# Activations kept in PSUM, and three weight remainders moved from VectorE to GpSimd

## What is computed

```python
# block 1 of the reference: 4 experts, the token id picks one
g = silu(h @ Wg[e].T); u = h @ Wu[e].T
y = (g * u) @ Wd[e].T            # kept where expert_ids == e
# block 2: 8 experts of 176, a router picks two
topk_s, topk_i = top_k(h @ Wg.T, 2); probs = softmax(topk_s)
y += w[..., e] * ((silu(h @ W1[e].T) * (h @ W2[e].T)) @ W3[e].T)
```

## Time and profile before

| | before |
|---|---|
| median of 3 runs | 164.85 us |
| the profiled execution's own time | 164.04 us |
| its span | 162.2 us |
| TensorE busy | 154.5 us (95%) |
| VectorE busy | 111.7 us (69%) |
| ScalarE busy | 67.8 us (42%) |
| GpSimd busy | 57.2 us (35%) |

### The profile page before, as it was taken

How to read it: one execution, slowest core, us unless ns; L and a number is a source line. 1 busy time by engine, 2 the same in 40 slices (tenths; PEclk the granted TensorE clock), 3 DMA queues, 4 the chain that set the end, 5 groups by cost and what they waited for, 6 DMA issues and landing times.

```text
span 162.2 us, 2463 instructions
## 1 busy us (share of the span) xinstructions
PE 154.5 (95%) x904; PEld 131.0 (81%) x904; DVE 111.7 (69%) x224; ACT 67.8 (42%) x121; POOL 57.2 (35%) x50
## 2 busy tenths in 40 slices
PE   7999899899999999999999799999999999999991
PEld 2477698789897788888889488888888888888890
DVE  0878999785986756799999947917444744444453
ACT  3385775754618622474335812324222222222210
POOL 0679956469767480555467310000000000000000
PEclk9999999999999999999999999999999999999999
DMA  3976353032030003033000000000000300000003
GB/s 107 349 246 191 82 203 107 0 97 76 29 97 0 2 0 101 0 97 97 0 4 0 0 0 2 4 0 0 0 0 4 129 0 0 0 2 4 0 0 129
DMA packets 4620, 8.76 MB, mean 54 GB/s; under 512 B 768, under 2 KB 1408, under 8 KB 4608
## 3 DMA queue, kind: packets, MB, share of 16 engines
q1 hardware_dynamic: 4176, 8.34, 16.3%
q10 hardware_dynamic: 432, 0.27, 0.5%
HBM read 7.55 MB, written 1.05 MB: 53 GB/s over the span
## 4 chain that ended last, share of the span: by engine, by line
PE 65%; DVE 21%; issue 4%; ACT 4%; POOL 3%; DVEq 0%; ACTq 0%; POOLq 0%
PE z L685 36%; PE y L710 22%; DVE act L587 5%; PE z L720 4%; DVE act_lo L552 4%; DVE norm L485 2%; DVE w_lo L558 2%; POOL gated L337 2%; DVE stats L468 2%; DVE hT_lo L492 1%; ACT act_hi L388 1%; ACT silu L416 1%; POOL rstd L299 1%; PE y L627 1%; DVE x_sb L498 1%
## 5 line engine op out<-in xcount | busy, mean ns | idle before, releaser
L685 PE MATMUL z<-hT_hi,w_hi 128*128 128x512 f32 x120 | 47.4, 395 | 1.1 <-ACT hT_hi L362 0.9
L685 PE MATMUL z<-hT_hi,w_lo 128*128 128x512 f32 x120 | 47.1, 393 | 0.0
L710 PE MATMUL y<-w_hi,act_lo 128*128 128x256 f32 x152 | 43.5, 286 | 1.0 <-DVE act_lo L552 0.9
L552 DVE TENSOR_TENSOR act_lo<-act,act_hi 128x512 fp32r<-128x512 f32 x38 | 33.6, 884 | 14.8 <-ACT act_hi L388 14.5
L710 PE MATMUL y<-w_hi,act_hi 128*128 128x256 f32 x152 | 43.0, 283 | 0.0
L710 PE MATMUL y<-w_lo,act_hi 128*128 128x256 f32 x152 | 42.9, 283 | 0.0
L416 ACT ACTIVATE silu<-z 128x512 f32<-128x512 f32 x38 | 22.6, 595 | 41.1 <-PE z L685 41.1
L685 PE MATMUL z<-hT_lo,w_hi 128*128 128x512 f32 x120 | 37.3, 392 | 0.0
L289 POOL TENSOR_TENSOR w_lo<-raw,w_hi 128x768 fp32r<-128x768 f32 (+1 forms) x15 | 27.5, 1845 | 20.3 <-ACT w_hi L353 18.9
L388 ACT CAST act_hi<-act 128x512 fp32r<-128x512 f32 x38 | 23.4, 617 | 19.7 <-DVE act L587 19.4
L710 PEld LDWEIGHTS y<-w_hi,act_lo 128*128 128x128 f32 x152 | 29.0, 191 | 3.2 <-DVE act_lo L552 1.5
(11 more groups left out here) (52 smaller groups left out, 80.8 us busy)
## 6 DMA issues: line engine op xcount, KB each, us to landing
raw<-weights_dram SPq DMA_DIRECT2D x11, 384.0 KB, 3.1
raw<-weights_dram SPq DMA_DIRECT2D x8, 256.0 KB, 4.5
x_sb<-x_dram SPq DMA_DIRECT2D x4, 256.0 KB, 4.4
out_dram<-x_sb SPq DMA_DIRECT2D x2, 256.0 KB, 2.5
out_dram<-x_sb SPq DMA_DIRECT2D x2, 128.0 KB, 2.0
out_dram<-x_sb ACTq DMA_DIRECT2D x2, 128.0 KB, 2.1
consts_sb<-consts_dram SPq DMA_DIRECT2D x1, 68.0 KB, 3.7
ids_sb<-token_ids_dram ACTq DMA_DIRECT2D x1, 4.0 KB, 3.9
```

The costliest lines, as they stand in the source:

```text
L552: nc.vector.tensor_tensor(act_lo[:, i, :], act[:, i, :], act_hi[:, i, :].bitcast(F32), ALU.subtract)\
L685: return nc.tensor.matmul(bank[:], w[b][:, c, cols], tokens[:, h, k, :], **flags)
L710: last = nc.tensor.matmul(o, a[:, q % BUFFERS, rows], w[b][:, c, wd], start=(first and j == 0), stop=(c == CHUNKS[b] - 1 and j == 2), skip ...
```

## The change

- Block b = 0: act(q) is written over its z bank in PSUM, and act_hi and act_lo read it from there.
- Block b = 1: gated(q) is written over the second z bank, and act(q) reads it there; act(q) itself stays in SBUF.
- The waits of up(q) follow: in b = 0 and for q = 16 and 17 it waits for act_lo in place of act (up(16) for act_lo(13), up(17) for act_lo(15)), and from q = 18 on for act(q-2) in place of silu and gated.
- On VectorE act_lo(15) moves ahead of gated(16).
- The remainders of w (0,5), (0,6) and (0,7) are taken by GpSimd and no longer by VectorE.
- rstd for the second half of b = 0 is computed by GpSimd in step 2, not 1.
- The router product for the second half of b = 1 stands behind down(20), not ahead of it.

```diff
-    "inverse_deviation": (1, 3, 4),
+    "inverse_deviation": (2, 3, 4),
-    "scores": (None, (7, 0), (7, 0)),
+    "scores": (None, (7, 0), (7, 1)),
-VECTOR_LO = ((0, 0), (0, 5), (0, 6), (0, 7))
+VECTOR_LO = ((0, 0),)
+        def act_place(q):
+            return z_banks(q)[0][:] if STEPS[q][0] == 0 else act[:, q % BUFFERS, :]
-                nc.scalar.copy(act_hi[:, q % BUFFERS, :], act[:, q % BUFFERS, :]).then_inc(act_hi_done, 1)
+                nc.scalar.copy(act_hi[:, q % BUFFERS, :], act_place(q)).then_inc(act_hi_done, 1)
-                nc.vector.tensor_tensor(act_lo[:, i, :], act[:, i, :], act_hi[:, i, :].bitcast(F32), ALU.subtract)\
+                nc.vector.tensor_tensor(act_lo[:, i, :], act_place(q), act_hi[:, i, :].bitcast(F32), ALU.subtract)\
+                if q == FIRST[1, 0]:
+                    act_low(q - 1)
                 if b == 1:
...
-                    nc.vector.tensor_tensor(gated[:, i, :], gate[:, h, :], z_banks(q)[1][:], ALU.mult)\
+                    nc.vector.tensor_tensor(z_banks(q)[1][:], gate[:, h, :], z_banks(q)[1][:], ALU.mult)\
                         .then_inc(gated_done, 1)
-                if q >= 1:
+                if q >= 1 and q != FIRST[1, 0]:
                     act_low(q - 1)
...
-                factor = z_banks(q)[0][:] if b == 0 else silu[:, i, :]
-                nc.vector.tensor_tensor(act[:, i, :], gated[:, i, :], factor, ALU.mult).then_inc(act_done, 1)
+                factors = (gated[:, i, :], z_banks(q)[0][:]) if b == 0 else (z_banks(q)[1][:], silu[:, i, :])
+                nc.vector.tensor_tensor(act_place(q), *factors, ALU.mult).then_inc(act_done, 1)
...
                 if q >= len(z) and b == 0:
-                    pe.wait_ge(act_done, q - len(z) + 1)
+                    pe.wait_ge(act_lo_done, q - len(z) + 1)
                 elif b == 1 and q < FIRST[1, 0] + 2:
-                    pe.wait_ge(act_done, 2 * q - FIRST[1, 0] - 2)
+                    pe.wait_ge(act_lo_done, 2 * q - FIRST[1, 0] - 2)
                 elif b == 1:
-                    pe.wait_ge(silu_done, q - 1)
-                    pe.wait_ge(gated_done, q - 1)
+                    pe.wait_ge(act_done, q - 1)
```

## The result

The changed kernel takes 167.49 us (median of 4 runs, 166.56 to 168.08), the kernel before 164.75: a ratio of 1.0167, 95% interval 1.011 to 1.0224. It is slower, and 167.49 lies 0.2 us from the predicted 167.7. The sum behind that number holds errors of opposite sign, and that the two numbers lie so close is partly luck, as the rows show.

A forecast was written before the change was run, and what follows sets the result against it. TensorE was taken to bound the kernel, so only its idle time could change. Terms -0.2, +0.8, +2.75, +0.7 and -1.15 summed to +2.9 us on 164.04, or 166.9; with 0.8 for the median 167.7, range 165.9 to 169.2.

The forecast's parts named there:

- R2: Rival: TensorE's clock falls after the pauses before up(17) and up(18), half speed losing 1.9 us: 169.6; chance 0.08.
- (c): Before up(17): it waits for act_lo(15), which stands behind the router's work on VectorE: +2.75 us, 2.6 to 2.95.
- (d): Before up(18): it waits for act(16) in place of gated(16): +0.7 us, bounds 0.6 to 0.8.
- (e): Later up-projections of block 1 wait for act(q-2), with time to spare: cost 0, at most 0.3 us.
- (f): Second router product: its move behind down(20), or an earlier hT_lo, removes the pause there: -1.15 us with the restart.
- (b): Block 0: added pieces make GpSimd set the pace, new pauses before down(3) and the token transposes: +0.8 us at up(8).
- (a): Block 0's activation in PSUM: act_lo never blocked, 0.69 us; -0.8 us before down(1), -0.2 before down(11).
- R1: Rival: GpSimd is not the pace in block 0, both new pauses vanish: sum +1.2 us, 166.1; chance 0.13.
- R3: Rival: VectorE's freed port pays for everything, early pauses vanish and router work shrinks: down to 163.8 us; chance 0.03.
- R4: Rival: the wait before up(17) isn't real, act_lo(15) being done before the router: +0.15 us, 165.0; chance 0.04.

The follow-up runs named there:

- e4: Changed kernel, but VectorE takes the remainders of w (0,5), (0,6), (0,7) again and GpSimd's rstd stands in step 1: 165.85 us, ratio 1.007.
- e8: Kernel before, nothing in PSUM; only act_lo(15) ahead of gated(16), and up(16) and up(17) waiting for act_lo: 168.82 us, ratio 1.0272.
- e6: e5 with gated of block b = 1 in SBUF again, up(q) waiting for silu and gated: 160.94 us, ratio 0.9812.
- e7: e5 with the second router product ahead of down(20) again: 161.47 us, ratio 0.984.
- e10: The changed kernel unaltered, measured a second time: 168.02 us, ratio 1.0227.
- e3: Changed kernel with 12 discarded warm-up matmuls on TensorE in the pause ahead of up(17): 166.21 us, ratio 1.0093.
- e11: e8 with 12 discarded warm-up matmuls in the pause ahead of up(17): 166.76 us, ratio 1.0141.
- e1: Changed kernel, but act(15) stays in its SBUF tile, so up(17) waits for act(15) again: 163.37 us, ratio 0.9922.
- e2: Changed kernel, but act_hi(15) ahead of tanh on ScalarE and act_lo(15) ahead of best_two on VectorE: 163.23 us, ratio 0.9915.
- e5: Changed kernel with the edits of e2 and e4 together: 161.87 us, ratio 0.9859.
- e9: Kernel before, with only the three remainders of w moved to GpSimd and rstd in step 2: 165.34 us, ratio 1.0053.

## Why the prediction was right

The number was right, and so were the largest term and the direction. One of its own signs of being wrong came true all the same: matmuls after the long pause stand 0.43 us apart (R2 below). By its own steps:

- **(c), the wait before up(17): right.** Predicted +2.75 us; the start moved by 2.84 in the profile, the idle time is 2.67 or 2.68 in the four profiles that have it (changed kernel twice, e4, e8), and e8 shows it with nothing else changed. What carried it was reading two orders against each other: up(17) waits for act_lo(15), which stands behind work that itself waits for transposes behind up(16).
- **(d), up(18): right.** Predicted +0.7; 0.56 in the profile, and e6 takes 0.73 back by the chain (0.93 by the medians).
- **(e) right at 0**: no pause after up(18). **(f) right**: -1.15 predicted, -1.17 measured from up(18) to the end, and either edit alone does it (e6, e7).
- **(b), GpSimd's load: the mechanism was right, half of its effect was not there.** Walked: gated(3) to 23.6, act(3) at 23.6, a pause of 0.9 before down(3). Measured: gated(3) ends at 24.1, or at 23.8 in e10, whose up(0) starts at 9.94; the idle time is 1.07 on the weight loads, and from up(6) to up(7) it is 3.72 us against 2.82, 0.90 more. But the second pause, at the token transposes, did not come. I had norm and GpSimd's gated(6) meet with gated(6) first; norm was first (VectorE's timeline, then GpSimd's):

```profile
27.21 1.54 DVE L489 TENSOR_SCALAR norm<-x_sb,mv,rstd 128x256 f32<-128x256 f32 x2
```

```profile
26.99 1.29 POOL L341 TENSOR_TENSOR gated<-silu,gate 128x512 f32<-128x512 f32 x1 [0.42 <-ACT silu L420]
28.50 1.40 POOL L341 TENSOR_TENSOR gated<-silu,gate 128x512 f32<-128x512 f32 x1 [0.22 <-ACT silu L420]
```

 The two norm operations end at 28.75, ahead of the transposes' turn. The text named this as open by 0.1 us and took half of it. From up(7) to up(8) it put some +0.7 us, and it is +0.23 (4.68 against 4.45, in e10 too).
- **(a), PSUM in block 0: under-sized.** I gave it -0.8 and -0.2. The -0.2 for the pause before down(11) counted its idle time alone; from up(8) to up(16) the changed kernel takes 24.54 us against 25.07, in both profiles, so -0.53. With the pieces left on VectorE (e4) up(16) starts at 55.48 where it was 56.92, although that execution's up(0) came 1.0 later: at least -1.4, since the pause before up(8) goes too. That pause stays, as forecast, with the pieces on GpSimd (0.83 us). Taken together, (a) and (b) were put at +0.6 up to up(16) and came to +0.05, and in e10's profile to -0.26. The mis-sized terms are the half of the second pause and the down(11) term.
- **R2, the falling clock: given 8 in 100, and it is what happens most of the time.** It was priced at 1.9 us, half speed over the 3.8 us of two pauses; the clock took 1.57 in the profile, and nothing at up(18). The sum left this term out. The argument against it, that the clock stayed full over pauses of 0.6 to 1.1 us, says nothing of a pause of 2.7. Over the kernels with the unfilled pause (changed kernel twice, e4, e8) 17 of 23 executions show a clock of 0.99 or less; with the pause filled (e3, e11) none of 12, without it (e1, e2, e5, e6, e7) none of 25. Why it falls in most executions and not in the others stays open.

In the profiled execution the errors add up as follows: +2.9 forecast, block 0 -0.55, (c) +0.09, (d) -0.14, the restart and the clock behind the long pause +1.82, (f) -0.02, in all +4.1. They do not cancel there. Against the kernels before beside them the medians are +2.74 (167.49) and, with the same code, +3.77 (e10). That the first lies so near +2.9 is partly luck: two of its four executions kept the full clock, and block 0 was put too high. The executions with a full clock, 166.56, 167.27 and 167.17, are what the sum of +2.9 was about; they lie 1.8 to 2.9 us over the kernel before beside them. Of R1 half is true: one of the two new pauses is absent, the other is there, and e4 and e9 show what GpSimd's load costs. R3 did not hold (the router's work is as long as before, 60.27 to 63.77), nor did R4.

An operation of VectorE with two SBUF inputs is held up beside GpSimd again, 1.83 us in e4 and 2.37 in e6 against 0.69. The Trainium skill, "GPSIMD Engine Reference", section 1 (Specifications), names contention with such instructions, and these rows agree. Taking them off the port is worth over a microsecond in block 0 (e4); in b = 1 it is worth the router product's pause (e7), and nothing once that product has moved (e6). The small variance operation, with one SBUF input, is held up too (1.33 against 0.16, e8). VectorE writing PSUM takes 0.69 to 0.70, as assumed.

## What to carry to other kernels

Where a result is written over its input in a PSUM bank, the bank is free one reader later. Find who reads last, and what stands ahead of that reader in its engine's order: a wait that costs nothing in the steady loop cost 2.8 us at the one step where other work stands in between, and moving the reader and the rounding ahead of it (e2) turned a loss of 1.7% into a gain of 0.85%. Take the parts of such a change apart: here block 0 in PSUM gains, the router product's move gains what gated in PSUM would gain alone, and three parts (the pieces on GpSimd, gated in PSUM beside that move, the order of act_lo) lose.

## What the runs showed of the hardware

- After a pause of 2.67 us on TensorE the next matmuls ran at 1.2 GHz for a while in 17 of 23 executions, which costs some 1.6 us beside the pause and the restart (up(17) 4.57 us in the changed kernel, 3.00 in e4's profile after the same pause). The slow level began behind the first matmul in one profile and more than a microsecond later in another (e10: from 65.8 us, the pause ended at 64.2). Twelve matmuls with a discarded result in the pause prevented it each time (e3 and e11, 12 executions).
- An operation on 128x4 values can cost VectorE 1.33 us instead of 0.16. In e3, e8 and e9 it starts at 14.16 to 14.25, about when GpSimd turns to its second gated product, and ends with that product (e8: 15.49 and 15.47); in the kernel before it starts at 14.11 and slips in ahead. With code that is the same up to there, this delayed up(16) by 0.70 us (e8 against the kernel before).
- The same kernel before takes one of two times, about 164.0 to 164.3 or 164.8 to 164.9 us (11 executions beside e9), with no difference in the code. The variance operation can make such a step. The warm-up shows another: its 24 matmuls took 7.23 us in one execution and 8.07 in another, so up(0) starts at 10.04 or 10.88 (e11, with the later start, has up(16) at 57.52, 0.60 later):

```profile
1.17 8.07 PE z L727 x24
```

 Whether one of them, or both, makes the two times was not tested.
